# The gathers of a tile issued in groups of seven, with a wait for their landing between groups

## What is computed

```
offset = (h @ w_off + b_off).reshape(N, H, W, GROUP, P, 2)
mask = softmax((h @ w_msk + b_msk).reshape(N, H, W, GROUP, P))
samp = bilinear_sample(img, iy, ix, Hin, Win)        # 4 corners of each of the 36 places
y = einsum('nghwpc,nhwgp->nhwgc', samp, mask) @ w_out + b_out
x = x + gamma1 * layer_norm(y); x = x + gamma2 * layer_norm(mlp(x))
t = t + attention(_ln(t)); t = t + experts(_ln(t), top 2 of 8)
```

## Time and profile before

| | |
|---|---|
| device time, median of 3 runs | 8874.52 us |
| span of the profiled execution | 14589.8 us |
| own time of the profiled execution | not given beside its span |
| GpSimd (POOL) busy | 6510.0 us, 45% of the span |
| TensorE busy | 5727.1 us, 39% |
| VectorE busy | 5562.0 us, 38% |
| ScalarE busy | 3113.0 us, 21% |
| DMA | 626.11 MB, mean 43 GB/s |

### The profile page before, as it was taken

One profiled execution on the slowest core, in us unless ns is written; L12 is line 12 of the kernel. 1 busy time (PEld: TensorE's weight loads), 2 busy tenths in 40 slices (PEclk: granted clock), 3 DMA queues, 4 the chain that ended last, 5 costly groups with the idle time before them and its releaser, 6 DMA issues.

```text
span 14589.8 us, 92590 instructions
## 1 busy us (share of the span) xinstructions
PE 5727.1 (39%) x24752; PEld 3652.5 (25%) x24752; DVE 5562.0 (38%) x11869; ACT 3113.0 (21%) x7121; POOL 6510.0 (45%) x6898
## 2 busy tenths in 40 slices
PE   3334344343433434334343333433435343442336
PEld 1112222222322223122232222312223222221224
DVE  3334334343343433434334343343433443333334
ACT  1112222222211222122221212212222121221123
POOL 5454444444444443454434444354443445445431
PEclk6666667666666667666666666766667666665667
DMA  4221112121121211212112121121211221111110
GB/s 72 50 48 39 45 41 44 45 45 43 39 45 43 44 43 36 50 43 45 41 38 46 42 46 41 37 51 42 47 41 36 49 42 48 37 38 45 43 35 13
DMA packets 851934, 626.11 MB, mean 43 GB/s; under 512 B 551018, under 2 KB 734562, under 8 KB 851472
## 3 DMA queue, kind: packets, MB, share of 16 engines
q0 software_dynamic: 221200, 452.62, 11.5%
q1 hardware_dynamic: 629600, 167.72, 7.3%
q10 hardware_dynamic: 672, 0.24, 0.0%
HBM read 549.46 MB, written 70.57 MB: 42 GB/s over the span
## 4 chain that ended last, share of the span: by engine, by line
another core or an unknown queue 33%; PE 24%; issue 23%; DVE 14%; ACT 5%; DMA 1%; SPq 0%; DVEq 0%; ACTq 0%
PE bank L1542 4%; PE bank L1508 3%; PE bank L1682 3%; PE bank L1594 3%; PE bank L1659 2%; PE bank L1432 2%; DVE y L1047 2%; PE bank L1517 2%; PE bank L1472 1%; ACT arena L838 1%; DVE ring L1037 1%; ACT xflat L789 1%; DVE nwt L955 1%; DVE cmax L1156 1%
## 5 line engine op out<-in xcount | busy, mean ns | idle before, releaser
L708 POOL DMA_INDIRECT ring<-column_table,idx_r x6860 | 6486.4, 946 | 7804.9 <-DMA wts_r<-corner_weight 5723.4
L1542 PE MATMUL bank<-v,pT 112*112 112x128 f32 x6496 | 995.9, 305 | 1865.8 <-issue 952.5
L1047 DVE TENSOR_REDUCE y<-ring 128x128 f32<-128x4608 f32 (+1 forms) x196 | 1572.3, 8022 | 16.8 <-remote 12.0
L1542 PEld LDWEIGHTS bank<-v,pT 112*112 112x112 f32 x6496 | 916.3, 202 | 2144.6 <-issue 1156.1
L1489 PE MATMUL bank<-ident,xn 112*128 112x112 f32 x224 | 55.3, 402 | 3369.7 <-remote 1866.9
L1508 PE MATMUL bank<-kT,qT 128*112 128x448 f32 (+3 forms) x1792 | 933.8, 618 | 786.2 <-issue 463.7
L1037 DVE TENSOR_TENSOR ring<-ring,bank 128x4608 f32<-128x4608 f32 (+1 forms) x196 | 970.0, 4949 | 120.8 <-remote 78.4
L1156 DVE TENSOR_REDUCE cmax<-arena 112x1 f32<-112x448 f32 (+3 forms) x896 | 504.4, 574 | 1121.7 <-ACT arena L820 709.6
L1489 PEld LDWEIGHTS bank<-ident,xn 112*128 112x128 f32 x224 | 37.1, 217 | 3379.5 <-issue 2511.2
L1517 PE MATMUL bank<-ident,arena 112*112 112x112 f32 x3248 | 547.6, 294 | 769.3 <-ACT arena L838 548.3
L802 ACT ACTIVATE xnT<-bank 128x448 f32<-128x448 f32 x56 | 30.4, 543 | 3628.1 <-issue 2168.4
(11 more groups left out here) (176 smaller groups left out, 8202.5 us busy)
## 6 DMA issues: line engine op xcount, KB each, us to landing
ring<-column_table,idx_r POOLq DMA_INDIRECT x6860
xflat<-dense_rows SPq DMA_DIRECT2D x56, 406.0 KB
column_table<-proj SPq DMA_DIRECT2D x196, 112.0 KB
corner_weight<-wts_s SPq DMA_DIRECT2D x56, 252.0 KB
wts_r<-corner_weight SPq DMA_DIRECT2D x196, 72.0 KB
hT<-dense_rows SPq DMA_DIRECT2D x224, 56.0 KB
tin<-tokens SPq DMA_DIRECT2D x56, 224.0 KB
out<-xn SPq DMA_DIRECT2D x56, 224.0 KB
```

What stands on the lines that cost most here:

```text
L708: pool.indirect_dma_start(ring[:, r, e * CORNERS:(e + 1) * CORNERS, :].rearrange("p s c -> p (s c)"), None, source, bass.IndirectOffsetOnA ...
L1047: dve.tensor_reduce(y[:, k % BLK % 2].rearrange("p (g c) -> p g c", g=G), ring[:, bass.ds(t % RING, 1)].rearrange("p o (g e) c -> p (o g) ...
L1542: ins = pe.matmul(bank[1][0:TT, 0:C], pT[:, c % 2, t], v[:, NT * c + t], start=(c == 0 and t == 0), stop=(c == j and t == nt - 1))
```

## The change

GpSimd issues the 35 gathers of a tile in five groups of seven. After each group it waits until all that has been issued into this buffer has landed, and counts up a new semaphore, `pool_passed`. After the fifth group the tile is complete and `tile_ready` is counted up at once. The deferred wait after the sixth gather of the next tile and the wait after the loop are gone, and VectorE waits for `t + 1` in place of `t + 2`.

```
+AT_ONCE = 7
...
+            def landed(r, count):
+
+                return 16 * count + (PRIMED if r == RING - 1 else 0)
...
                             source, bass.IndirectOffsetOnAxis(ap=idx_r[:, r, e:e + 1], axis=0),
                         ).then_inc(gathered[r], 16)
-                        if e == 5:
-
-
-                            if r:
-                                pool.wait_ge(gathered[r - 1], q * (16 * FETCHED) + 16 * FETCHED)
-                            else:
-                                pool.wait_ge(gathered[RING - 1], q * (16 * FETCHED) + PRIMED)
-                            pool.sem_inc(tile_ready, 1)
+                        if e % AT_ONCE == AT_ONCE - 1:
+                            pool.wait_ge(gathered[r], q * (16 * FETCHED) + landed(r, e + 1))
+                            pool.sem_inc(pool_passed, 1)
+                    pool.sem_inc(tile_ready, 1)
...
-            pool.wait_ge(gathered[RING - 1], 16 * FETCHED * (TILES // RING) + PRIMED)
-            pool.sem_inc(tile_ready, 1)
...
-                dve.wait_ge(tile_ready, t + 2)
+                dve.wait_ge(tile_ready, t + 1)
```

More of the change, by code:

```diff
@@ L231, in build @@
         passed = sem("passed")
+        pool_passed = sem("pool_passed")
         table_zeroed = sem("table_zeroed")
```

## The result

The changed kernel takes **11,433.7 us** (median of 4 runs, 11,428.6 to 11,446.5) against 8,872.7 us before: 28.9% slower, ratio 1.2887 with a 95% interval of 1.2868 to 1.2905. The direction was forecast; the size was not. 2,561 us were added where 1,715 were expected, and the time lies 534 us above the top of the range.

The account below looks back on a forecast made before the run. GpSimd's issue of gathers was taken to bound the kernel. Each of 980 waits was to take 2.2 + 0.8 = 3.0 us, 1.75 more than now: 8,874.5 + 1,715 = 10,590 us, range 10,200 to 10,900.

Parts of the forecast that it names:

- The bound: On GpSimd: its issue of gathers sets the pace of the measured runs, 8,568 us or 97% of the time.
- two equal stretches: Two 15 us trace windows: GpSimd busy 11.34 us with 13 gathers in both, however much the other engines work.
- 1.249 us a gather: On GpSimd: distance between gather starts, taken for unrecorded runs too; 6860 gathers make 8,568 us.
- the 102 us that my sum left open: Whole kernel before: start, gathers, last landing and end sum to 8,773 us, 1.1% short of the median.
- Step one: Across each new wait: start of the group's last gather to its landing, 2.2 us, at least 1.9.
- dear waits: Rival at the new waits: SyncE's transfers delay the seventh landing 0.5 us each, 11,080 us in all; chance 0.08.
- Step two: Across each new wait: landing to GpSimd's next gather start, 0.8 us, bounds 0.7 to 1.0, count-up included.
- The old wait: Wait at the next tile's sixth gather: its data had landed long before, 4.3 us in all, so removal gains nothing.
- The range's top: Whole kernel: 10,900 us, the upper bound plus 0.1 us of crowding for each wait.
- The ring: Tile buffers: don't become short; multiply, sum and reload take 16 us against three tiles of 52.5 us each.
- faster: Rival: short bunches free transfer engines, so other engines' loads and stores come sooner; 102 us less, 8,773 us; chance 0.02.
- the forecast profile: Changed kernel's trace: span near 14,590 us, GpSimd busy near 6,510, 980 waits, weight wait down about 1,715 from 5,723.

Follow-up runs that it names:

- the kernel with 34: Kernel before the change with 34 gathers a tile in place of 35: 8,645.3 us against 8,877.5, ratio 0.9737.
- the new record: Kernel before the change, unchanged, recorded once more: 8,876.0 us, span 8,874.2 us.
- a wait one group behind: Against the kernel before: the same 980 waits and count-ups, each asking for the previous group's landing: 8,933.2 us, ratio 1.0065; on the 14,589 us chip 14,434.8 us.

## Why the prediction was right or wrong

**The bound.** Right, for the chips on which the metric was taken: GpSimd's gathers set the pace, shown by the kernel with 34. The reason that I gave for setting the span aside was wrong. The unexplained 56% of the earlier trace rows was not made by the recording: it is a real condition, in which the kernel truly takes 14.6 ms, 24 times out of 24 on one chip. The two equal stretches of the earlier trace rows, read as proof of GpSimd's independence, fit that condition: one lies late in a row of gathers and the other at the start of one.

**1.249 us a gather.** Right: on the new record the mean distance is 1.26 us, its own few waits included. The longer distances (79 us in all) and a program's end of 177 us from the last gather, where I had 152, are the 102 us that my sum left open.

**Step one, landing 2.2 us.** Right for the typical one (7015.0 less 7012.8), wrong for the mean. I took one landing, on an idle queue, for 980. The rival "dear waits" named SyncE's transfers and gave them 0.08. The step that failed is the one that set the forecast's delay of the seventh landing to nothing, "both queues together leave over 80% of the transfer engines idle": that is a mean over time, and the stores come in 56 bursts that fill nearly all of them for some 10 us. With waits every 11.5 us each burst meets one. This term, priced at 0, is 464 us for the 75 longest, 416 of them beside a burst, and 98 for the rest. My own sign for "dear", a distance above 3.5 us, is met by the mean (3.92) and missed by the median (3.35).

**Step two, restart 0.8 us.** Mis-sized: 1.1 to 1.2 us. The earlier trace rows allowed 0.7 to 1.0, and I chose near the bottom; the count-up adds 0.08, and two further ones at every fifth wait more. The typical distance is 3.35 us where I had 3.0: 0.35 x 980 = 343 us.

**The sum with what was measured**: 980 x (3.35 - 1.25) = 2,058; tail 464 + 98; less the old waits (31 us above an ordinary gap) and the shorter end (24) make 2,565 us against 2,561.

**The rest.** The old wait was not free but cost about 30 us on the path; my 4.3 us came from an execution in which the other engines stood still through much of each row of gathers, so that little disturbed the landings. The range's top added 0.1 us of crowding a wait; it needed 0.57. The ring did hold. The fit that the Trainium skill gives ("DMA: Bandwidth & Descriptors", Anatomy of one DMA) makes 2.15 us for the transfer with its completion, as an estimate; the typical trace agrees (2.2 until the data are through) and says that a restart of 1.1 us comes on top.

**The rival "faster"** was put at 0.02 and priced at 102 us. It did not happen where the metric was taken, and on another chip it did, with 3,126 us (14,506 less 11,380). Its sign came true there, but not its reason: transfer engines left free in between can hardly be what helps where they are 80% idle in the unbroken row. I had the stalls before me in the earlier trace rows and explained them away. In the forecast profile, the span of 14,590 us was wrong for the same reason; the busy time (6,525 us) and the count of waits came out as said. The wait for weights, forecast to fall by about 1,715 us, fell from 5,723 to 76, and to 31 already in the new record of before.

## What to carry to other kernels

On an engine that sets the pace, a wait on a just issued gather costs the round trip of one gather each time, here 2.1 us above the ordinary spacing, plus every burst of small stores that it happens to meet; a wait one group behind costs nearly nothing (56 us for 980) and is enough where only a bound on what is in flight is wanted. Price a new wait by the spread of the thing waited for, beside the densest traffic of the other queues, and not by one clean instance or by a mean share. And where a record's span is far from the measured time, record again before arguing why.

## What the runs showed of the hardware that was not expected

- Chips differ. One gave 14,589 and 14,506 us (medians of 17 and 7 runs in two sessions) for the kernel whose medians are 8,873 to 8,889 us elsewhere; from some 10 us into an unbroken row of gathers 1.25 us apart the other engines stand still for most of the time. Why is open. Breaking the row after 7 gathers, with a wait for their landing, removes it (11,380 us), after 12 most of it (11,153 us); waits that don't block do not (14,435 us). The times after 12 gathers and with waits that don't block are single runs.
- Three stores of a front, one of them in 2,688 pieces of 4 bytes, keep the transfer engines almost fully busy (DMA share 1.06 and 0.88) at 76 and 81 GB/s for most of the 12.7 us that the last takes to land. The gather beside them is followed by the next after 12.85 us in place of 3.3, so it landed some 9.5 us late; making the 4-byte store twice adds 4.7 us a burst.
- GpSimd needs 1.1 us from the end of the data to its next gather after a blocked wait, with one count-up between, and 0.08 us more for each further one, while gathers in a row cost 1.25 us from start to start.
